# A four-layer cross-attention kernel: the steps, loads and bias sums of its prologue arranged anew

## The reference

```python
# layer 0
Mn = Wn @ inorm(x) + bn ; Mm = Wm @ inorm(c) + bm          # per batch, over tokens
A  = softmax(Mn^T Mm) ; x = Wo @ ((Wl @ c + bl) A^T) + bo + x
# layers 1 and 2
a = layer_norm(c) * gamma + beta
Q = x @ Wq.T ; K = a @ Wk.T ; V = a @ Wv.T                 # 16 heads
x = x + tanh(gate) * (softmax(mask(Q K^T / 4)) V) @ Wo.T
# layer 3
x = x + alpha * (softmax((x Wq^T)(c Wk^T)^T / 16) (c Wv^T)) Wo^T
```

## Time and profile before

| | us |
|---|---|
| median of three runs | 613.49 |
| lowest, highest | 611.21, 613.78 |
| the profiled execution | 610.86 |
| its span, first to last instruction | 609.1 |

### The profile page before, as it was taken

One profiled execution on the slowest core, in us unless ns is written; L12 is line 12 of the kernel. 1 busy time (PEld: TensorE's weight loads), 2 busy tenths in 40 slices (PEclk: granted clock), 3 DMA queues, 4 the chain that ended last, 5 costly groups with the idle time before them and its releaser, 6 DMA issues.

```text
span 609.1 us, 26470 instructions
## 1 busy us (share of the span) xinstructions
PE 564.9 (93%) x11059; PEld 494.9 (81%) x11059; DVE 470.7 (77%) x1055; ACT 469.8 (77%) x993; POOL 121.8 (20%) x132
## 2 busy tenths in 40 slices
PE   2579999999999999999999999999999999999975
PEld 1468897988888887988888888888888888888864
DVE  5675969878796969878797969878797869877555
ACT  2589969868788878868788878969788778978662
POOL 3502161100701052100701043100701034000000
PEclk9989999999999999999999999999999999999979
DMA  5520000210020100210020100210011100010001
GB/s 127 191 65 13 3 3 3 76 38 2 3 76 2 37 3 2 76 37 2 3 75 4 37 2 3 76 37 2 2 40 39 37 2 3 3 36 3 2 2 36
DMA packets 18501, 18.35 MB, mean 30 GB/s; under 512 B 1828, under 2 KB 18340, under 8 KB 18404
## 3 DMA queue, kind: packets, MB, share of 16 engines
q1 hardware_dynamic: 17880, 16.42, 8.4%
q0 software_dynamic: 320, 0.26, 0.4%
q10 hardware_dynamic: 204, 0.14, 0.1%
HBM read 12.63 MB, written 4.19 MB: 28 GB/s over the span
## 4 chain that ended last, share of the span: by engine, by line
PE 77%; ACT 10%; DVE 5%; issue 4%; SPq 2%; DMA 1%; DVEq 0%; ACTq 0%
PE psum L391 14%; PE psum L676 11%; PE psum L393 11%; PE psum L392 11%; PE psum L730 8%; PE psum L723 5%; ACT work L853 5%; PE psum L643 4%; PE psum L656 3%; PE psum L471 2%; PE psum L483 2%; PE psum L528 1%; PE psum L667 1%; ACT v L802 1%; PE psum L560 1%
## 5 line engine op out<-in xcount | busy, mean ns | idle before, releaser
L1057 DVE TENSOR_TENSOR shifted<-psum,negmax 128x512 f32<-128x512 f32 x128 | 88.5, 691 | 5.3
L1053 DVE TENSOR_REDUCE negmax<-psum 128x8 f32<-128x512 f32 x128 | 87.3, 682 | 5.6 <-PE psum L656 5.5
L867 ACT ACTIVATE work<-psum,group_mask 128x512 f32<-128x512 f32 x128 | 80.6, 703 | 10.4 <-PE psum L676 10.4
L676 PE MATMUL psum<-const,work 64*128 64x64 f32 x1536 | 65.8, 229 | 13.4 <-ACT work L853 9.6
L676 PEld LDWEIGHTS psum<-const,work 64*128 64x128 f32 x1536 | 55.7, 141 | 26.6 <-ACT work L853 15.5
L853 ACT ACTIVATE work<-shifted 128x512 f32<-128x512 f32 x128 | 74.5, 626 | 2.1 <-DVE shifted L1057 1.4
L730 PEld LDWEIGHTS psum<-v,work 128*64 128x64 f32 x2048 | 63.0, 138 | 7.7 <-issue 3.1
L730 PE MATMUL psum<-v,work 128*64 128x34 f32 x2048 | 67.6, 225 | 0.9 <-ACT work L867 0.9
L802 ACT ACTIVATE v<-psum 64x256 f32<-64x256 f32 x128 | 49.7, 388 | 18.7 <-PE psum L393 17.6
L848 ACT ACTIVATE work<-psum,negmax 128x256 f32<-128x256 f32 x128 | 50.6, 491 | 8.8 <-DVE negmax L1049 8.8
L1049 DVE TENSOR_REDUCE negmax<-psum 128x2 f32<-128x512 f32 x64 | 41.1, 683 | 14.9 <-PE psum L643 14.0
(11 more groups left out here) (181 smaller groups left out, 1524.4 us busy)
## 6 DMA issues: line engine op xcount, KB each, us to landing
x_raw<-in_x_dram SPq DMA_DIRECT2D x8, 512.0 KB, 4.3
...
```

What stands on the lines that cost most here:

```text
L676: mm_ = pe.transpose(banks[h][:, C * n:C * n + C], src[rows], ident[rows, rows])
L867: act.activation(probsT[:, at, :], o[:], ACT.Copy, scale=group_mask[:, 2 * i + c:2 * i + c + 1]).then_inc(free, 1)
L1053: dve.tensor_reduce(negmax[:, i % 2, :], sv, AX_X, ALU.max, negate=True).then_inc(rowmax, 1)
L1057: dve.tensor_tensor(shifted[:, i % 4, :].rearrange("t (j k) -> t j k", k=C), sv, negmax[:, i % 2, :].unsqueeze(2).broadcast_to([P, NJ, C]) ...
```

## The change

The transfers: ScalarE now issues the mask, the constants, the four layer-0 weights, the biases and `bo`; SyncE issues x, c, the mask row and the twelve weights directly behind them, layer 3 in the order o, q, k, v. Each of the twelve weights has a semaphore of its own.

The bias columns: VectorE sums the products of POOL with two reductions for each layer and forms `own_bias` with one product (`KB`, now on VectorE). `VB` is now 8 small products (weights 128x128, one column) of the split Wo with `v_bias`, which give `o_bias` directly, and VectorE copies the two columns. The wide copy, the row copy, POOL's second product and `OB` are gone.

The clearing: `v2` tiles are cleared and get their ones in new steps `CL.0` and `CL.1` of VectorE; PE waits for them ahead of `VB2`.

The tables `PE_FIRST`, `ACT_FIRST` and `DVE_FIRST` are new. Core of the diff:

```diff
-            for i, n in enumerate(("Wn", "Wm", "Wo", "Wl")):
-                sp.dma_start(w0_raw[:, i, :], ...).then_inc(w0_loaded, 16)
             sp.dma_start(mrow_u8[:].rearrange("r p k -> r (p k)"),
                          m_g[0].unsqueeze(0).broadcast_to([P, TOK])).then_inc(rows_loaded, 16)
-            sp.dma_start(bo_row, ...).then_inc(bo_loaded, 16)
-            for n in "qkvo":
-                sp.dma_start(raw[n + "1"][:], w_in(w[f"L1_xattn_W{n}"])).then_inc(w1_loaded, 16)
...
+            for l in (1, 2):
+                for n in "qkvo":
+                    sp.dma_start(raw[f"{n}{l}"][:], w_in(w[f"L{l}_xattn_W{n}"])).then_inc(raw_loaded[f"{n}{l}"], 16)
+            for n in "oqkv":
+                sp.dma_start(raw[n + "3"][:], w_in(w[f"L3_xattn_w_{n}"])).then_inc(raw_loaded[n + "3"], 16)
...
                 elif name in ("VB1", "VB2"):
                     l = int(name[2])
-                    pe.wait_ge(bias_step, 2 * l)
+                    pe.wait_ge(bias_summed, 3 * l - 1)
+                    parts = [(part[:, k, :].bitcast(F32), k) for part in wT[f"o{l}"] for k in range(NK)]
                     for m in range(NK):
-                        mm_ = pe.transpose(o[:, P * m:P * m + P], v_bias_wide[:, l - 1, m, :], ident)
+                        for n, (part, k) in enumerate(parts):
+                            mm_ = pe.matmul(o[:, m:m + 1], part[:, P * m:P * m + P], v_bias[:, l - 1, k:k + 1],
+                                            start=n == 0, stop=n == len(parts) - 1)
...
             for step in PE_PROLOGUE:
+                if step == ("P", "VB2", 0):
+                    pe.wait_ge(values_clear, 4)
...
+            def clear_values(i):
+
+                dve.memset(v2[i][:], 0.0).then_inc(values_clear, 1)
+                dve.wait_ge(values_clear, 2 * i + 1)
+                for h in range(2):
+                    ins = dve.memset(v2[i][C * h:C * h + C, :, :, h, VW - 1], 1.0)
+                ins.then_inc(values_clear, 1)
+
+            def bias_columns(l):
+
+                for n, bias in ((2 * l - 2, k_bias), (2 * l - 1, v_bias)):
+                    dve.wait_ge(kv_ready, n + 1)
+                    dve.reduce_sum(bias[:, l - 1, :], kv_product[:, n], AX_X).then_inc(bias_summed, 1)
+                dve.wait_ge(const_loaded, 16)
+                dve.wait_ge(bias_summed, 3 * l - 2)
+                dve.tensor_tensor(own_bias[:, l - 1], ..., parity..., ALU.mult).then_inc(bias_summed, 1)
...
-            for t in v2:
-                ins = dve.memset(t[:], 0.0)
-            ins.then_inc(cleared, 1)
```

More of the change, by code:

```diff
@@ L54 @@
 PE_FIRST = """
[L55 to L57 removed]
+    xT.0-1 MT.0 MS.0 Wq1.0 Wk1.0 cT.0-1 Wq2.0 GT.0 W0T.0 W0.0 Wv1.0 nT.0-1 Wo3T.0 Mn.0-1 Mm.0-1 Wo1.0 Wo2.0 M3.0 K1.0
+    S0.0-3 V0.0-1 VB1.0 T0.0-3 S0.4-7 Wk2.0 VW3.0 A0.0-3 T0.4-7 K1.1 A0.4-7 Wv2.0 VB2.0 Q1.0
 """
 ACT_FIRST = """
[L60 to L61 removed]
+    xT.0 Wq1.0 xT.1 cT.0-1 Wq2.0 Wk1.0 TG.0 NM.1 NM.0 Wv1.0 nT.0-1 Mn.0-1 Mm.0 Wo3T.0 Mm.1 Wo2.0 Wo1.0 M3.0 K1.0 X0.0-3
+    T0.0-3 Wk2.0 X0.4-7 VW3.0 T0.4-6 H.0 T0.7 Wv2.0 Q1.0 H.1 K1.1
 """
 DVE_FIRST = """
[L64 to L65 removed]
+    ST.0 MT.0 ST.1 MS.0 ST.2-3 MV.0 WB.0 GT.0 TG.0 W0T.0 NB.0 Wq1.0 cT.0 Wk1.0 cT.1 Wq2.0 W0.0 KB.1 Wv1.0 ON.0 nT.0-1
+    Mn.0-1 Mm.0-1 Wo2.0 Wo1.0 M3.0 S0.0-3 V0.0 VB1.0 V0.1 KB.2 CL.0 S0.4-7 Wk2.0 A0.1 A0.3 VW3.0 L.0 CL.1 Wv2.0 A0.5 A0.7
+    VB2.0 L.1
 """
@@ L568, in weight_step @@
                 name = step[1]
-                used = {"W0": ["W0T"], "MS": ["MT"], "VW3": ["Wo3T"]}.get(name, [])
+                used = {"W0": ["W0T"], "MS": ["MT"], "VW3": ["Wo3T"], "VB1": ["Wo1"], "VB2": ["Wo2"]}.get(name, [])
                 o, signal = start_fill(None, step, False, consumed=[("P", n, 0) for n in used])
@@ L953, in _ @@
                     weight_step(step)
-                elif step[0] == "KB":
-                    bias_columns(step[1])
-                elif step[0] == "OB":
-                    act.wait_ge(o_product_ready, step[1])
-                    for m in range(NK):
-                        row_sum(kv_product[:, 2 * step[1] - 1, m, :], o_bias[:, step[1] - 1, m:m + 1], tgates[:, step[1] - 1:step[1]])
                 elif step[0] == "NM":
@@ L1131, in weight_step @@
                     ins.then_inc(mask_turned, 1)
+                elif name in ("VB1", "VB2"):
+                    dve.tensor_copy(o_bias[:, int(name[2]) - 1, :], o[:, 0:NK]).then_inc(free, 1)
                 elif name == "GT":
```

80 lines of the change are left out of this document (27 added, 53 removed).

## The result

The changed kernel took 614.84 us (median of 20 runs, 612.41 to 617.85) beside 611.67 us for the kernel before on the same chip (20 runs, 609.71 to 616.39). The ratio is 1.0038, 95% interval 1.0025 to 1.0052. The forecast was 606.2 us, a ratio of 0.988. The profiled execution has a span of 612.8 us, against 609.1.

What follows compares the result with a forecast made beforehand. The prologue, held by SyncE's queue and VectorE, was taken to set S1.0, the loop's first score product: 17.5 + 12.6 + 24.0 = 54.1 us against 61.46, 7.4 gained, hence 606.2 us; range 602 to 610.5.

Steps and rivals of the forecast that it cites:

- ScalarE's queue: First stretch: five more loads issued before ScalarE's first copy, 0.7 to 2.9 us each; start expected at 9 us, harmless to 12.5.
- The spreading: First stretch: VectorE's two copies that spread the layer-0 weights, 1.93 us behind the moments, ending at 15.3 us.
- late-start rival: Start of the kernel: weights or constants land some 4 us later, or SyncE's queue stalls longer; gain 3.4, 610.1 us, chance 0.18.
- Wq2: First stretch: fifth 0.26 MB load, landing near 14.2 us, wanted by VectorE at 15.3; hidden with 1 us to spare.
- Gates and moments: First stretch: last gate load lands 5.4 us after issue, gates copy at 8.0 us, moments end at 13.4.
- `norm_bias`: First stretch, before c_norm: a partial collision with GpSimd's products, 0.6 us, bounds 0.1 (alone) and 1.3 (behind a whole product).
- Second stretch: From the start of c_norm to VectorE's first row maximum: TensorE runs without a gap, 12.6 us.
- Third stretch: From VectorE's first row maximum to S1.0, the loop's first score product: VectorE's list 21.8 us, then state_hi and K1.1; 24.0 us.
- second product: Third stretch: second small product for o_bias, at 18.2 us of the 24, 1.7 us (bounds 0.9 to 3.7), just not late for state_hi.
- the second slow phase would vanish: TensorE's clock after the mixed product: no pause, so the low-clock phase goes and TensorE is some 1.5 us shorter.
- PE or DVE leads: Third stretch: forecast had VectorE leading, 0.50; rival had TensorE leading, 21.8 us, gain 10.4, 603.1 us, chance 0.18.
- From S1.0 to the end: From the loop's first score product on: same code in both kernels, so the 548 us of before.

Runs made afterwards that it cites:

- e2: Kernel before with only the changed kernel's new transfers (five loads moved to ScalarE's queue); ratio 1.0041.
- e3: Changed kernel with the four layer-0 weights and bo issued by GpSimd instead of ScalarE; ratio 0.9919 to the kernel before.
- e9: e3 with both value tiles cleared in VectorE's early idle time and K1.1 moved ahead of Q1.0 on ScalarE; ratio 0.9869, 602.95 us.
- e10: e9 with the small layer-0 weights loaded once, to 64 partitions, on GpSimd's queue; ratio 0.9857, 603.04 us.
- e7: Changed kernel with both value tiles cleared in VectorE's idle time at the start, transfers as they are; ratio 0.9969.

## Why the prediction was wrong

- **ScalarE's queue: the step that failed.** "ScalarE issues five more loads before its first copy (0.7 to 2.9 us each, the two rows); its own work before `c_norm` is about 4.5 us, so it may start as late as 12.5 us without harm; I expect 9." Before, ScalarE started at 4.69 us, so 9 gives the five loads 0.86 us each, near the low end of the stated range; at its middle, 1.8 us, the start is at 13.7, past the 12.5. The five took 1.15, 0.73, 4.38, 2.88 and 0.41 us, 9.6 together, and the first bias load behind four of them 4.76, where it had taken 1.49 before. ScalarE started at 17.50 us and made its first copy at 18.79. e2 and e3 show this step from both sides: +0.4% with the new transfers alone, and 1.0038 to 0.9919 when only these five loads go to another queue.
- **The same loads as data.** The spreading was put right behind the moments, and the sum said nothing of the landing of what it spreads, nor of the biases that the gate transpose needs; only the late-start rival did. Wl landed at 22.9 us and `bl` at 23.4, and these two, not ScalarE's late arithmetic, held `c_norm` last. It is the same step: both wait for the same stalled queue.
- **Wq2 was sized too early** as well, hidden here and seen in e3, where it landed at 15.4 us against 14.2. The fourth weight landed 7.3 us after its issue (12.16 to 19.42); less four loads of 0.75 us that leaves 4.3 and not 3.7, and the same sum then gives 14.7.
- **Gates and moments.** The gates copy was at 9.06 us, not 8.0; the issue-to-landing time of the last gate load was 6.5 us, not 5.4. The moments ended at 14.7, not 13.4. Right but 1.3 us short, hidden behind Wl.
- **The late start was a rival**, and both of its signs showed: "ScalarE's first copy after 12.5 us, or the gate columns after 15.5" (18.79 and 23.81). Its size was taken as 4 us with a gain left; it was 7.9 us. No rival had the start so late that the change lost.
- **`norm_bias`** took 0.16 us, not 0.6. GpSimd's four products ran from 16.84 to 21.76 us, so by then they were over; in e3 and e9, where `c_norm` is early, it took 0.78 and 0.27 us, and in e10, 0.05 us behind the start of GpSimd's first product, 1.23 us. The bounds of 0.1 and 1.3 held.
- **Second stretch:** 12.8 us for 12.6. Right in sum; e7's 11.9 us for the same instructions shows that some 0.9 of it is TensorE's clock, which the sum did not name.
- **Third stretch:** 25.1 us for 24.0. VectorE's list took 21.2 us for 21.8 (the terms as listed add up to 20.9, and to 21.7 with the two waits of 0.4). The second product started 18.26 us after the first row maximum, forecast 18.2; each product took 1.9 us, forecast 1.7; K1.1 was last, with TensorE waiting 0.41 us. What was missing is the clock: "just not late for `state_hi`" fits the upper level, and from 58 to 62 us TensorE had the lower one, so the query copy came at 60.72 and pushed `state_hi` and K1.1 by 1.9 us. The statement that "the second slow phase would vanish" was wrong for this kernel, which had two low phases, and right for e7.
- **PE or DVE leads:** VectorE in the changed kernel, up to its last attention sum; TensorE once the clearings are gone and K1.1 is moved (e9).
- **From S1.0 to the end** the span is 549.6 us, not 547.6. The code is the same, and the stores of the groups follow each other in 69.3 us (131.43, 200.70, 269.96, 339.19 us; before 68.8, 69.2 and 69.3). The difference is in the last 36 us. From the last `state_lo` to the end, with 402 instructions of TensorE in each; before, after and e7:

```profile
573.57:609.10 35.53, 23.88 (x402) 20.20 (x400) 20.43 (x45) 15.91 (x33) 0.00 (x0) 0.88 0.05 16
```

```profile
575.61:612.80 37.19, 25.05 (x402) 21.65 (x400) 20.46 (x45) 16.16 (x33) 0.00 (x0) 0.85 0.05 16
```

```profile
571.64:611.20 39.56, 27.52 (x402) 23.83 (x400) 20.53 (x45) 16.15 (x33) 0.00 (x0) 0.76 0.05 15
```

The same work takes 35.5, 37.2 and 39.6 us, at a granted clock of 0.88, 0.85 and 0.76. Over the last 34 us the clock was 0.87, 0.83 and 0.73, and S1.0 to the end 547.6, 549.6 and 552.3 us. In the profiles of all the kernels here these two go together: at 0.86 to 0.87 it was 547.6 to 547.9 us, at 0.81 to 0.84 549.4 to 550.7, at 0.78 to 0.79 550.6 to 551.2.
